# Attention phases of a two-block transformer kernel: ScalarE writes the head-masked Q and K from PSUM, inputs are double-buffered, and TensorE's loop holds two groups

## The reference

```
x = LN(x + attn(x, x, x, causal));  x = LN(x + attn(x, ctx, ctx));  x = LN(x + moe(x))   # block 0
x = x + attn(LN(x), LN(ctx), LN(ctx));  x = x + gelu(LN(x) @ w1 + b1) @ w2 + b2          # block 1
attn: Q, K, V = q@wq+bq, k@wk+bk, v@wv+bv; softmax(Q K^T / sqrt(8)) V @ wo + bo
```

## Time and profile before

| | us |
|---|---|
| runs, median (lowest, highest) | 1685.31 (1680.41, 1690.23) |
| profiled execution, its own time | 1670.39 |
| its span, first to last instruction | 1668.7 |
| TensorE / VectorE / ScalarE / GpSimd busy | 1314.3 / 1063.7 / 879.8 / 894.5 |
| mean granted TensorE clock | 0.89 |

### The profile page before, as it was taken

One profiled execution on the slowest core, in us unless ns is written; L12 is line 12 of the kernel. 1 busy time (PEld: TensorE's weight loads), 2 busy tenths in 40 slices (PEclk: granted clock), 3 DMA queues, 4 the chain that ended last, 5 costly groups with the idle time before them and its releaser, 6 DMA issues. The chain is left out here.

```text
span 1668.7 us, 60930 instructions
## 1 busy us (share of the span) xinstructions
PE 1314.3 (79%) x23128; PEld 1073.4 (64%) x23128; DVE 1063.7 (64%) x2513; ACT 879.8 (53%) x1496; POOL 894.5 (54%) x1424
## 2 busy tenths in 40 slices
PE   2899999999999663979999994111128999994898
PEld 0677877777888562669999994011115788883676
DVE  1677777778788408957777774565646778872000
ACT  0587877778888500023333332345445888873333
POOL 0376766666676400077777773666613667663111
PEclk9999999999999955989999997555557999997899
DMA  3133333233332160012222222455532233321333
GB/s 88 55 95 101 95 99 103 85 95 103 101 94 88 46 202 26 0 45 61 61 61 60 61 62 67 114 146 153 159 106 84 90 101 94 107 83 34 112 109 93
DMA packets 174602, 147.63 MB, mean 88 GB/s; under 512 B 21168, under 2 KB 137392, under 8 KB 174512
## 3 DMA queue, kind: packets, MB, share of 16 engines
q1 hardware_dynamic: 166064, 129.11, 25.7%
q0 software_dynamic: 8448, 17.32, 4.4%
HBM read 95.45 MB, written 50.86 MB: 88 GB/s over the span
## 5 line engine op out<-in xcount | busy, mean ns | idle before, releaser
L743 DVE TENSOR_REDUCE at_mx<-at_ps_s 128x16 f32<-128x1024 f32 x128 | 156.1, 1220 | 105.6 <-PE at_ps_s L492 60.9
L1320 POOL DMA_INDIRECT ex_xg<-x,ex_ti x136 | 165.2, 1215 | 46.8 <-issue 44.6
L1372 ACT ACTIVATE ex_xt<-ex_ps_x 128x128 f32<-128x128 f32 x136 | 37.7, 277 | 268.8 <-PE ex_ps_x L1332 154.8
L1349 PE MATMUL ex_ps_y<-ex_wt,ex_hg 128*128 128x128 f32 x1088 | 157.2, 288 | 2.6 <-ACT ex_hg L1380 2.6
L680 ACT ACTIVATE at_pt<-at_ps_t 128x1024 f32<-128x1024 f32 x128 | 130.5, 1020 | 53.1 <-PE at_ps_t L506 52.3
L673 ACT ACTIVATE at_pr<-at_dd 128x1024 f32<-128x1024 f32 x128 | 135.1, 1056 | 35.4 <-DVE at_dd L751 35.3
L751 DVE TENSOR_TENSOR at_dd<-at_ps_s,at_mx 128x1024 f32<-128x1024 f32 x128 | 153.7, 1202 | 0.1
L1532 POOL DMA_INDIRECT cb_yg<-rows,cb_sl x128 | 125.5, 981 | 45.2 <-issue 44.8
L1349 PEld LDWEIGHTS ex_ps_y<-ex_wt,ex_hg 128*128 128x128 f32 x1088 | 131.6, 191 | 26.0 <-ACT ex_hg L1380 22.1
L1340 PE MATMUL ex_ps_h<-ex_xt,ex_wt 128*128 128x128 f32 x1088 | 146.4, 278 | 0.0
L506 PE MATMUL at_ps_t<-ident,at_pr 128*128 128x128 f32 x1024 | 139.2, 279 | 4.9 <-issue 4.2
(11 more groups left out here) (258 smaller groups left out, 3438.0 us busy)
## 6 DMA issues: line engine op xcount, KB each, us to landing
rows<-ex_y SPq DMA_DIRECT2D x136, 64.0 KB
x<-at_ln_out SPq DMA_DIRECT2D x32, 256.0 KB, 3.2
at_kx<-in_xt SPq DMA_DIRECT2D x16, 256.0 KB, 2.8
at_qx<-in_xt SPq DMA_DIRECT2D x16, 256.0 KB, 2.8
at_vin<-in_xt SPq DMA_DIRECT2D x16, 256.0 KB, 2.7
at_xr<-in_x SPq DMA_DIRECT2D x16, 256.0 KB, 2.9
x1t<-at_xt SPq DMA_DIRECT2D x16, 256.0 KB, 3.3
at_kx<-in_ctxt SPq DMA_DIRECT2D x16, 256.0 KB, 2.7
```

The costliest lines, as they stand in the source:

```text
L743: dve.tensor_reduce(mx[:, p], ps_s[:, :, 4 * p:4 * p + 4, :], AX.X, ALU.max).then_inc(mx_ready, 1)
L1320: pool.indirect_dma_start(out=xg[:, s, :], out_offset=None, in_=x_src, in_offset=bass.IndirectOffsetOnAxis(ap=ti[:, s:s + 1], axis=0)).the ...
L1349: mm = pe.matmul(ps_y[s % 2][:, :], hg[:, s % 2, f, :], wt[:, s % HB, W2 + D * f:W2 + D * f + D], start=(f == 0), stop=(f == FC - 1))
```

## The change

ScalarE's `copy_k` and `copy_q` become `mask_k` and `mask_q`: two activations each, straight from `ps_g` into `kb` and `qb`, with the 0/1 column as scale and the bias times that column (`side`, made once on VectorE) as bias. The functions of GpSimd and the buffers `kt`, `qt` go. `kb`, `qb`, `qx`, `ot`, `c.vx` and the layer norm's `out` get a second buffer; `kx` and `vin` become one `kv` with two, loaded once. V is projected one group ahead (g+1 in step g, V of group 0 in the prologue). TensorE uses `over_pairs`: per layer five passes over two groups; written out are groups 0 to 3, 14 to 19, 30, 31 (0 to 3, 14, 15 in the last phase). The waits follow the new names. The diff, cut to its core:

```diff
-        kx = n.sb("kx", [P, GT])
-        vin = n.sb("vin", [P, GT])
-        qx = n.sb("qx", [P, GT])
+        kv = n.sb("kv", [P, 2, GT])
+        qx = n.sb("qx", [P, 2, GT])
         xr = n.sb("xr", [P, 2, GP, D])
         xb = n.sb("xb", [P, 2, GP, D])
-        kt = n.sb("kt", [P, 2, GT])
-        qt = n.sb("qt", [P, 2, GT])
-        kb = n.sb("kb", [P, 2, GT])
-        qb = n.sb("qb", [P, GB, 2, SEQ])
+        kb = n.sb("kb", [P, 2, 2, GT])
+        qb = n.sb("qb", [P, 2, GB, 2, SEQ])
+        side = n.sb("side", [P, nl, 4])
...
-                def load_q(a):
+                def load_kvq(a):
                     lay = layers[a.layer]
-                    if beyond(a.g, 0):
-                        sp.wait_ge(q_ready, a.g)
+                    if beyond(a.g, 1):
+                        sp.wait_ge(v_ready, a.g - 1)
+                        sp.wait_ge(k_ready, a.g - 1)
+                    sp.dma_start(kv[:, a.u, :], lay.kv_src[:, bass.ts(a.place, GT)]).then_inc(in_kv[a.u], 16)
+                    if beyond(a.g, 1):
+                        sp.wait_ge(q_ready, a.g - 1)
                     if lay.chained:
                         sp.wait_ge(tr_out[a.u], 16 * (a.k - NG // 2 + 1))
-                    sp.dma_start(qx[:, :], lay.q_src[:, bass.ts(a.place, GT)]).then_inc(in_q, 16)
-
-                def load_k(a):
-                    if beyond(a.g, 0):
-                        sp.wait_ge(k_ready, a.g)
-                    sp.dma_start(kx[:, :], layers[a.layer].kv_src[:, bass.ts(a.place, GT)]).then_inc(in_k, 16)
-
-                def load_v(a):
-                    if beyond(a.g, 0):
-                        sp.wait_ge(v_ready, a.g)
-                    sp.dma_start(vin[:, :], layers[a.layer].kv_src[:, bass.ts(a.place, GT)]).then_inc(in_v, 16)
+                    sp.dma_start(qx[:, a.u, :], lay.q_src[:, bass.ts(a.place, GT)]).then_inc(in_q[a.u], 16)
...
                 def step(a):
                     if a.shift(2).exists():
-                        load_q(a.shift(2))
-                    if a.shift(3).exists():
-                        load_k(a.shift(3))
-                    if a.shift(1).exists():
-                        load_v(a.shift(1))
-                    if a.shift(2).exists():
+                        load_kvq(a.shift(2))
                         load_x(a.shift(2))
                     if a.shift(-2).exists():
                         store(a.shift(-2))
-                over_pairs(sp, step, nl, 2)
+                over_pairs(sp, step, nl)
...
-                    pe.wait_ge(kb_ready, quad + 1)
-                    pe.wait_ge(qb_ready, quad + 1)
+                    if h == 0:
+                        pe.wait_ge(kb_ready, a.g + 1)
+                        pe.wait_ge(qb_ready, a.g + 1)
                     if beyond(quad, 0):
                         pe.wait_ge(d_ready, 2 * quad)
...
                 def project_k(a):
-                    pe.wait_ge(in_k, 16 * a.g + 16)
-                    pe.matmul(ps_g[:, :], layers[a.layer].wk[:, :], kx[:, :], start=True, stop=True).then_inc(k_ready, 1)
+                    pe.wait_ge(in_kv[a.u], 16 * (a.k + 1))
+                    pe.matmul(ps_g[:, :], layers[a.layer].wk[:, :], kv[:, a.u, :], start=True, stop=True).then_inc(
+                        k_ready, 1)
...
-                pe.wait_ge(qt_ready, 1)
+                pe.wait_ge(qb_ready, 1)
+                project_v(a0)
+                scores(a0, 0)
+                pe.wait_ge(vx_ready, 1)
                 project_k(a0.shift(1))
                 pe.wait_ge(bvb_ready, 1)
-                pe.wait_ge(kt_ready, 2)
+                pe.wait_ge(kb_ready, 2)
...
-                        pe.wait_ge(qt_ready, g + 2)
+                        pe.wait_ge(qb_ready, g + 2)
                         project_k(a.shift(2))
                     if prior:
                         values(a.shift(-1), 1)
-                    if more:
-                        pe.wait_ge(kt_ready, g + 3)
-                    elif a.shift(1).exists():
-                        pe.wait_ge(qt_ready, g + 2)
-                    else:
-                        pe.wait_ge(y_ready, g - 1)
-                    project_v(a)
+                    if following:
+                        if more:
+                            pe.wait_ge(kb_ready, g + 3)
+                        else:
+                            pe.wait_ge(qb_ready, g + 2)
+                        project_v(a.shift(1))
                     turn(g * 2, 0, 1)
-                    if a.shift(1).exists():
+                    if following:
                         scores(a.shift(1), 0)
                     if beyond(g, 1):
-                        pe.wait_ge(vx_ready, g + 1)
+                        if following:
+                            pe.wait_ge(vx_ready, g + 2)
+                        else:
+                            pe.wait_ge(y_ready, g - 1)
                         turn_x(a.shift(-2))
...
-                over_single(pe, step, nl)
+                over_pairs(pe, step, nl)
...
-                def copy_k(a):
+                def mask_k(a):
+
                     act.wait_ge(k_ready, a.g + 1)
                     if beyond(a.g, 1):
-                        act.wait_ge(kb_ready, 2 * a.g - 2)
-                    act.activation(kt[:, a.u, :], ps_g[:, :], ACT.Identity, bias=layers[a.layer].bk[:, 0:1]).then_inc(
-                        kt_ready, 1)
-
-                def copy_q(a):
+                        act.wait_ge(s_ready, 2 * a.g - 2)
+                    for j in range(2):
+                        ins = act.activation(kb[:, a.u, j, :], ps_g[:, :], ACT.Identity,
+                                             bias=side[:, a.layer, 2 + j:3 + j], scale=c.side[:, 2 + j:3 + j])
+                    ins.then_inc(kb_ready, 1)
+
+                def mask_q(a):
+
                     act.wait_ge(q_ready, a.g + 1)
                     if beyond(a.g, 1):
-                        act.wait_ge(qb_ready, 2 * a.g - 2)
-                    act.activation(qt[:, a.u, :], ps_g[:, :], ACT.Identity, bias=layers[a.layer].bq[:, 0:1]).then_inc(
-                        qt_ready, 1)
+                        act.wait_ge(s_ready, 2 * a.g - 2)
+                    for f in range(2):
+                        ins = act.activation(qb[:, a.u, :, f, :], ps_g[:, :].rearrange("p (b q) -> p b q", b=GB),
+                                             ACT.Identity, bias=side[:, a.layer, f:f + 1], scale=c.side[:, f:f + 1])
+                    ins.then_inc(qb_ready, 1)
 
                 def copy_v(a):
 
                     act.wait_ge(v_ready, a.g + 1)
-                    if beyond(a.g, 0):
-                        act.wait_ge(pv_ready, 2 * a.g)
+                    if beyond(a.g, 1):
+                        act.wait_ge(pv_ready, 2 * a.g - 2)
...
+                    for f, b in enumerate((lay.bq, lay.bq, lay.bk, lay.bk)):
+                        ins = dve.tensor_tensor(side[:, i, f:f + 1], b[:, 0:1], c.side[:, f:f + 1], ALU.mult)
+                ins.then_inc(side_ready, 1)
+                for i, lay in enumerate(layers):
                     ins = dve.tensor_copy(bvb[:, i, :], lay.bv[:, 0:1].broadcast_to([P, P]))
                 ins.then_inc(bvb_ready, 1)
-                dve.wait_ge(kt_ready, 1)
-                for j in range(2):
-                    ins = dve.tensor_scalar(kb[:, j, :], kt[:, 0, :], c.side[:, 2 + j:3 + j], None, ALU.mult)
-                ins.then_inc(kb_ready, 2)
...
-                def mask_k(a, h):
-
-                    cols = slice(GT // 2 * h, GT // 2 * h + GT // 2)
-                    pool.wait_ge(kt_ready, a.g + 1)
-                    if beyond(a.g, 0):
-                        pool.wait_ge(s_ready, a.g * 2 + h - 1)
-                    for j in range(2):
-                        ins = pool.tensor_tensor(kb[:, j, cols], kt[:, a.u, cols],
-                                                 c.side[:, 2 + j:3 + j].broadcast_to([P, GT // 2]), ALU.mult)
-                    ins.then_inc(kb_ready, 1)
-
-                def mask_q(a, h):
-
-                    cols = slice(GT // 2 * h, GT // 2 * h + GT // 2)
-                    pool.wait_ge(qt_ready, a.g + 1)
-                    if beyond(a.g, 0):
-                        pool.wait_ge(s_ready, a.g * 2 + h - 1)
-                    for f in range(2):
-                        ins = pool.tensor_tensor(qb[:, QB * h:QB * h + QB, f, :],
-                                                 qt[:, a.u, cols].rearrange("p (b q) -> p b q", b=QB),
-                                                 c.side[:, f:f + 1, None].broadcast_to([P, QB, SEQ]), ALU.mult)
-                    ins.then_inc(qb_ready, 1)
```

More of the change, by code:

```diff
@@ L95, in shift @@
         return At(self.layers, self.g + d, self.layer, self.place + d, (self.u + d) % 2, self.k + (self.u + d) // 2)
[L98 to L107, removed]
 def over_pairs(eng, step, layers, tail=1):
@@ L148, in __init__ @@
         self.zg = n.sb(name + "_zg", [P, 2, GP, D])
-        self.out = n.sb(name + "_out", [P, GP, D])
```

(34 more changed lines are left out.)

66 lines of the change are left out of this document (27 added, 39 removed).

## The result

The changed kernel takes 1721.23 us (median of 4 runs, 1717.20 to 1728.94) against 1687.07 us of the kernel before on the same chip (4 runs, 1680.41 to 1690.23): ratio 1.0213, 95% interval 1.0165 to 1.0262, slower by 34.2 us. Forecast were 44.3 us and 1730.

What follows compares the result with a forecast made beforehand. It took TensorE's own instruction stream as the bound. Terms 50.7 + 0 - 4.2 - 2.2 + 0 + 0 gave +44.3 us, on the median 1685.3 a forecast of 1730; range 1706 to 1796, to hold 8 in 10.

Steps and rivals of the forecast that it cites:

- part 2: ScalarE's queue: masking activations delay V, leaving TensorE holes of 1.08 us (self) and 1.37 (cross, last); 50.7 us.
- One end of the range: ScalarE's queue before V: a step of 0.80 everywhere, holes of 1.48 and 1.77 us, 67 us.
- part 3: TensorE's two-group loop: fewer back jumps -4.2 us, more first-run code partly hidden in the hole; term 0, from -4 to +8.
- parts 4, 5: V one group ahead, with prologue: -2.2 us and 0 within 2; double buffers and single K and V input load: 0.
- Rival B: TensorE's loops: two-group body does not stay in instruction memory; 4 us at each of 12 back jumps, 48; chance 0.30.
- The ninth block: TensorE's instruction memory: two groups span seven or eight blocks with waits, and one fetched ahead would be the ninth.
- Rival C: Ahead of V: K pair ends before TensorE finishes the values, no hole, not slower; 1679 to 1687 us; chance 0.12.

Runs made afterwards that it cites:

- e4: Changed kernel with a third K activation, into a buffer nobody reads, ahead of the two; ratio 1.0433 to the kernel before.
- e9: Changed kernel with constant 1.0 instead of the 0/1 column as scale of the mask activations; ratio 1.0194 to the kernel before.
- e7: e2 with 230 empty waits at the start of combine, moving the last phase's loop; ratio 1.0057 to the kernel before.
- e8: The changed kernel itself, run again beside others on one chip; 1719.44 us, ratio 1.0225 to the kernel before.
- e3: Changed kernel with layer-norm scalings and K masks ahead of a copy of transposes in ScalarE's queue; ratio 1.0082 to the kernel before.
- e11: e10 with 330 instead of 230 empty waits ahead of the combine phase; ratio 1.0194 to the kernel before.
- e5: e1 with 120 and 256 empty waits in TensorE's program, so its loops lie elsewhere; 1699.65 us, ratio 1.0101 to the kernel before.
- e1: Kernel before with only TensorE's driver changed, to loops over two groups; ratio 1.0311 to the kernel before.
- e6: Changed kernel with 180 empty waits (90 instructions) ahead in TensorE's program; 1803.19 us, ratio 1.0713 to the kernel before.
- e2: Changed kernel with the K and Q masks put back on GpSimd; ratio 1.0203 to the kernel before.
- e10: e7 with K masked by ScalarE as in the changed kernel, Q masks still on GpSimd; ratio 1.0490 to the kernel before.

## Why the prediction was right, and where it was not

**The hole (part 2).** Right in place and mechanism, and near in size as a wait. Forecast were 50.7 us; measured 0.91 to 0.96 in self, 1.23 in cross and last, 45.2 in 39 steps. V came 8.53 us after the transpose, not 8.75, since the pair's step is 1.32 to 1.33, not 1.40 (an activation is 0.78, not 0.80, and overlaps the next by 0.11), and V follows the K pair by 0.05, not 0.13. That periods in the loops carry a hole in full was right (e4, e9). One end of the range was mis-added: a step of 0.80 puts three times 0.10 ahead of V, not four, so holes of 1.38 and 1.67, 63 us and not 67.

**What the masks cost as timed.** e7 and e8, same chip, both with their loops kept, differ by the masks (and by where their code lies): 1693.38 and 1719.44, so 26.1 us, half of the forecast and not 45.2. The loops carry the hole nearly in full: a step of e7 takes 16.06 us in self and 15.60 in cross, of the changed kernel 16.95 and 16.70. The steps written out do not. TensorE's idle for issue in the middle of bursts, over both phases, is 26.1 us in e7 and 11.0 and 12.0 in the two executions of the changed kernel: 14 to 15 of the 19 us. The traces read as if ScalarE ran on while TensorE waits for code, so that such a stall ahead of V costs nothing as long as there is a hole to fall into; no run tests this alone. The prediction said this for its part 3 but took it into the loop's price; it belongs to the hole's too. In e9 the same idle is 19.5 us, which takes 8 of the 15.4 by which K's waits fell, and it is a part of why e3 and e11 disappointed.

**The loop (part 3).** The mis-sized term beside the hole. -4.2 us were forecast for fewer back jumps. In e5, the two-group loop alone, steps (from one copy into `at_xt` to the next) alternate between 15.53 and 15.91 in cross, mean 15.72, which is the mean before (15.65, 15.79); in self 15.82 and 16.38, mean 16.10, against 16.24. So the cross loop saves nothing, the self loop 0.14 a step. In cross two idles stand in every pass of e5 where the kernel before has 0.19 at each of two jumps:

```profile
504.17 0.63 PE L568 MATMUL at_ps_g<-ident,at_ln_out 128*128 128x128 f32 x4 [0.28 <-POOL at_ln_out L208]
...
509.38 1.09 PE L508 MATMUL at_ps_t<-ident,at_pr 128*128 128x128 f32 x8 [0.28 <-ACT at_pr L675]
```

The one jump left costs 0.28 to 0.33, and 0.23 to 0.28 go to a wait for GpSimd's layer norm that was not there. The larger miss is first-run code: its idle in bursts, over both phases, grows from 13.0 us before to 25.5 in e5, where the prediction had 8.5 more, hidden in the hole. With it the loop alone costs 12.4 us in the phases and 14.7 on the clock (e5, 1699.65 against 1684.92), against the -4 to +8 forecast. Beside the hole, that cost is mostly hidden (11.0 and 12.0, above).

**V ahead, buffers, prologue (parts 4, 5).** Forecast -2.2 and 0. e7 without the masks is at +10.3 and e5 at +12.4 in the phases: -2 (-6.3 in the medians; neither is known to better than some 5 us). Without its hole a step of the changed kernel takes 16.95 - 0.93 = 16.02 us in self and 16.70 - 1.23 = 15.47 in cross, where it took 16.24 and 15.72; these 0.2 a step, some 9 us in 38 steps, weren't forecast as such. In two cross steps TensorE's idle beside the hole is 0.28 us (one jump) where it was 0.54 (two jumps of 0.19, two of 0.08 ahead of V), so half of it is the back jumps' saving; which edit brings the rest was not tried.

**Sum.** Forecast 44.3; 32.7 and 36.4 in the phases of two executions, 34.2 timed. Taken apart by medians on one chip: the loop +14.7 (e5), V ahead and buffers -6.3 (e7 against e5), the masks +26.1 (e8 against e7), together 34.5. The forecast had -4.2, -2.2 and 50.7. That the sum is near is partly luck: a loop 19 too cheap and masks 25 too dear have opposite signs.

**Rival B** had chance 0.30, and did not happen: 86 packets, no idle of several us. But it is a true mechanism. Its idle at the jump was priced well (4 us; 3.7 to 4.1 in e1, 5.0 to 5.6 in e6), its whole price too low, 9.6 to 12.7 us a miss, and the number of misses too high, eight of twelve in e6: 84 us in all against up to 62. The ninth block that the prediction suspected fits the nine packets of a miss. The kernel escapes it by where its loops lie: by the borders that fit the runs, its self loop begins just behind one and its last loop ends 10 to 22 instructions ahead of one. **Rival C** is refuted: no step of the loops runs without the hole.

Nothing run here beats the kernel before. The nearest are e7 (1.0057) and e3 (1.0082).

## What to carry to other kernels

Before work moves onto an engine that is "only 53% busy", walk its queue from the event that starts it in each step to the result that the bounding engine waits for: what is added in that stretch, beyond its slack, is added to the period of a steady loop, whole, and the same work put elsewhere in the queue may cost much less (e3, 1.0082 against 1.0213). When a loop's body on TensorE comes near the size of the instruction memory, count the instruction packets of the queue: more of them than the code has blocks means that it is fetched again, in every pass or every second, and then code that isn't even in the loop can decide the time. Two costs that fall into the same wait are not additive, and neither is what is won by removing one.

## What the hardware showed that was not expected

- A loop of 6.4 to 6.7 blocks of 256 instructions is kept or fetched anew depending on its start: moving it by 50 instructions took a phase from 350.8 to 300.1 us (e10, e11), by 90 instructions a kernel from 1719.44 to 1803.19 (e8, e6).
- At a missed back jump TensorE idles 3.7 to 6.3 us (3.75 to 4.10 in e1, 4.99 to 5.60 in e6, 6.05 and 6.28 in e2), and 8.0 to 8.6 in e10; nine packets are fetched, and the whole cost is 9.6 to 12.7 us.
- First-run TensorE code in bursts of small matmuls stands still for up to 2.2 us at a time even when nothing is fetched twice (e5, e7), 25.5 and 26.1 us in all.
- ScalarE's 128x512 activation from PSUM: 0.598 us plain, 0.67 to 0.685 with a bias per partition (before, e9), 0.78 with scale too; back to back they overlap by 0.10 to 0.12.
